# Cross-attention's transposes, copies and PV one slot later, its probabilities in eight buffers over self-attention's space, and some weight pieces split sooner

## The chip, the core and the metric

The kernel runs on one core of one Trainium2 chip. The metric is the device time in microseconds of one execution; lower is better. Engines are TensorE (PE; its weight loads are PEld), VectorE (DVE), ScalarE (ACT), GpSimd (POOL) and the SyncE queue (SP), which starts most transfers.

## What is computed

One decoder layer in float32 over 2048 tokens: x is (16, 128, 256), as is the context.

```python
x = x + attn(layernorm(x))            # heads of 64: 16; self-attention
x = x + xattn(layernorm(x), ctx)      # heads of 16: 16; one mask over 128 keys
x = x + ffn(layernorm(x))             # 8 experts, 256 -> 512 -> 256
```

`attn` and `xattn` are projections to Q, K and V, scores, a softmax over 128 keys, P times V, and an output projection. The feed-forward part runs **all** 8 experts for each token (GELU between the two products) and scales their sum by one number per token, `norm_g`, from an RMS-normed gate with a softmax and its maximum.

## The kernel before

Each core product is made of three matmuls with operands split in a high and a low half (`three`, L743): high times high, high times low, low times high. So every operand that TensorE reads in this way is first rounded by one engine (the "hi" step, mostly ScalarE) and its rest is computed by another (the "lo" step, VectorE or GpSimd).

The work has three phases: `ph` 0 is self-attention, 1 is cross-attention, 2 the experts. Each goes over 4 groups of 512 tokens. The two attentions are written as a **software pipeline by slots**: `run` goes through 16 slots per group, and in each slot every engine walks its own table (`PE_ORDER`, `ACT_ORDER`, `DVE_ORDER`, `POOL_ORDER`). An entry is a name, a kind of step and a lag in slots; `steps` says which jobs fall in which slot. The engines meet by semaphores only. A table has one row per kind of slot (self-attention, cross-attention, the mixed slots between them). Group g+1's first steps and the last steps of groups g-1 and g-2 run within group g's slots. After the last cross-attention group, `run` adds `DRAIN` slots in which the remaining steps are done, and the first experts' products (`up`) are set between them (`UP_AHEAD`).

In cross-attention a slot handles one quad of four (head, token tile) blocks. Its chain is:
- scores of the quad into one of two banks S0, S1 (L842 writes the mask, L849 adds the scores; `scores` waits for the exponentials of the quad before the last, `exped`);
- negated row maximum on VectorE (L1354), then the exponentials on ScalarE one slot later (L1176, four instructions, written to `probs`);
- reciprocal of the row sums on VectorE (L1359), multiplication on GpSimd (`normalise`, L1622, lag 2);
- four transposes on TensorE into bank T (L870, lag 3), copied back over the probabilities (L1363 on VectorE, lag 4);
- P times V for two quads at a time into bank O (L891, lag 5, odd quads only);
- after eight quads bank O is read with its bias (`out_sum`, L1385; the last time L1375 and L1378), split in halves (L1631, L1637 on GpSimd), projected into banks Y0, Y1 (`project_out`, L743, lag 6) and added to the tokens (`add_residual`, L1402).

The probabilities of both attentions lie in a ring of `RING` = 6 buffers (`probs`), so an exponential waits for the PV of six quads before. The experts' hidden tiles (`hid`) use four of these buffers as well, and the gate's logits (`LT`) lie in `qkv`, the space of self-attention's V, K and Q.

Weights come in pieces of 256 KB into four staging tiles `wst`. `weight_slots` says in which slot ScalarE rounds which piece (L1106); the low half is made by GpSimd one slot later (L1609), or, for pieces listed in `LOW_BY_DVE`, by VectorE at the end of the slot named there (L1320). A staging tile is loaded again when its piece is split. The first experts' pieces are handled likewise ahead of the experts' loop: `FIRST_EXPERTS` gives the slots of ScalarE's part (L1194), `FIRST_LOWS` those of GpSimd's (L1684); the others are split by VectorE (L1260) within the loop, seen from `LEAD` on.

The norm ahead of a cross-attention group is done by VectorE (statistics, L1264, L1272, L1275), GpSimd (`rstd`, L1617) and, from the second group on, ScalarE, which writes the normed tokens `xn` (L1166) in two pairs of tiles at the slots in `NORM1`.

The end of the drain matters here. For the last group the order is: PV of the last pair; then on TensorE the gate's logits (L1015) and one `up` product; on VectorE the two evacuations of bank O (L1375, L1378); then TensorE's last projection into Y0 and Y1, the residual (L1402) and the experts' loop. VectorE also makes the low halves of the first two hidden tiles (`LOW_AHEAD`, L1260, `PT<-probs`), which need ScalarE's high halves (L1238), which stand behind ScalarE's copy of the logits (L1206):

```python
            def weights(ph, g, n):
                if ph == 2 and n == 15:
                    for m in LOW_AHEAD:
                        hidden_lo(0, m)
```

It is called at the end of each slot, after VectorE's table.

## Time and profile before

| what | value |
|---|---|
| median of 3 runs | 831.58 us (830.26 to 831.97) |
| profiled execution, its own time | 830.68 us |
| its span, first to last instruction | 828.9 us |
| busy: PE, PEld | 809.5 us (98%), 702.8 us (85%) |
| busy: ACT, DVE, POOL | 484.7, 430.9, 231.0 us |
| granted clock of TensorE | 1.00 in all slices |

How to read it: self-attention runs to about 313 us, cross-attention from there to about 457 us, the experts to the end. Ends of matmuls are modelled, so TensorE's busy share tells less than the distances from one start to the next. In a row of the timeline the bracket at the end gives how long the engine had been idle before the instruction and who released it. The sums of waits are worth reading for TensorE only where it is the engine that ends last.

### The profile page before, as it was taken

What the parts mean: (1) busy time and instruction counts of PE and PEld (TensorE: products, weight loads), DVE (VectorE), ACT (ScalarE), POOL (GpSimd) and SP (SyncE); (2) the same over time, 40 slices, a digit from 0 to 9 for tenths busy, and PEclk for the clock granted to TensorE, in tenths of its full rate; (3) what the DMA queues carried; (4) which work ended last, traced back from release to release, by engine and by line L of the source; (5) the groups of instructions that cost most, each with busy time, mean ns of one, the idle gap of its engine ahead of it and who ended that gap; (6) DMA issues with size and microseconds to landing.
All of it is one profiled execution on the core that took longest, in us unless ns stands there. A gap on an engine that the chain in (4) does not pass through costs nothing.

```text
span 828.9 us, 16894 instructions
## 1 busy us (share of the span) xinstructions
PE 809.5 (98%) x6139; PEld 702.8 (85%) x6139; DVE 430.9 (52%) x918; ACT 484.7 (58%) x1552; POOL 231.0 (28%) x225
## 2 busy tenths in 40 slices
PE   9999999999999998999999999999999999999998
PEld 7778888888888887888887799989999899989997
DVE  4565475456547567989886545542234222432223
ACT  5556545545654567898987566554544554444543
POOL 3344333322342356787877000000000000000000
PEclk9999999999999999999999999999999999999999
DMA  6311000000000038666660433000000000000000
GB/s 189 120 52 40 1 2 2 1 2 1 1 19 10 1 74 163 134 147 141 148 142 16 114 89 92 24 27 1 1 1 14 13 0 0 0 26 1 1 1 26
DMA packets 21641, 38.02 MB, mean 46 GB/s; under 512 B 4152, under 2 KB 4672, under 8 KB 21568
## 3 DMA queue, kind: packets, MB, share of 16 engines
q1 hardware_dynamic: 20688, 36.45, 17.7%
q8 instruction: 46, 0.75, 0.4%
q10 hardware_dynamic: 880, 0.60, 0.2%
q14 instruction: 27, 0.22, 0.1%
HBM read 24.45 MB, written 6.29 MB: 37 GB/s over the span
## 4 chain that ended last, share of the span: by engine, by line
PE 87%; DVE 5%; ACT 2%; POOL 2%; issue 2%; SPq 1%; DMA 1%; POOLq 0%; ACTq 0%
PE Y L743 28%; PE A L743 27%; PE S L743 11%; PE T L870 6%; PE S L861 3%; PE O L904 3%; PE S L842 2%; PE O L891 2%; ACT probs L1176 2%; PE S L849 1%; PE S L972 1%; POOL probs L1622 1%; DVE probs L1363 1%; DVE nm L1354 1%; DMA arena<-arena 1%
## 5 line engine op out<-in xcount | busy, mean ns | idle before, releaser
L1176 ACT ACTIVATE probs<-S,nm 128x128 f32<-128x128 f32 x512 | 180.9, 384 | 119.7 <-DVE nm L1354 119.7
L743 PEld LDWEIGHTS Y<-arena,PT 128*128 128x128 f32 x1536 | 199.6, 191 | 11.1 <-DVE PT L1260 1.7
L1260 DVE TENSOR_TENSOR PT<-probs,PT 128x512 fp32r<-128x512 f32 x128 | 88.7, 693 | 230.1 <-ACT PT L1238 230.1
L743 PE MATMUL Y<-arena,PT 128*128 128x256 f32 x1536 | 204.2, 283 | 0.4
L1622 POOL TENSOR_TENSOR probs<-probs,rinv 128x512 f32<-128x512 f32 x128 | 133.9, 1047 | 208.3 <-DVE rinv L1359 208.2
L743 PE MATMUL A<-XT,arena 128*128 128x512 f32 x612 | 159.2, 394 | 0.0
L1238 ACT ACTIVATE PT<-probs 128x512 fp32r<-128x512 f32 x128 | 80.8, 631 | 102.9 <-PE Y L743 102.5
L743 PEld LDWEIGHTS A<-XT,arena 128*128 128x128 f32 x612 | 108.2, 189 | 18.0
L1363 DVE COPY probs<-T 128x512 f32<-128x512 f32 x96 | 66.0, 687 | 107.6 <-PE T L870 107.2
L1176 ACT ACTIVATION_READ_ACCUMULATOR probs<-S,nm 128x1 f32 x512 | 114.1, 223 | 0.0
L743 PE MATMUL S<-XT,arena 128*128 128x512 f32 x384 | 99.7, 395 | 1.7 <-DVE arena L1260 1.7
L1354 DVE TENSOR_REDUCE nm<-S 128x4 f32<-128x512 f32 x128 | 84.0, 677 | 13.2 <-PE S L849 10.7
L870 PE MATMUL T<-ident,probs 128*128 128x128 f32 x512 | 78.3, 275 | 4.8 <-POOL probs L1622 3.2
L743 PEld LDWEIGHTS S<-XT,arena 128*128 128x128 f32 x384 | 68.2, 189 | 13.6 <-issue 1.8
L870 PEld LDWEIGHTS T<-ident,probs 128*128 128x128 f32 x512 | 58.6, 140 | 24.3 <-POOL probs L1622 14.9
L743 PE MATMUL Y<-arena 128*128 128x256 f32 x480 | 76.1, 295 | 3.0 <-issue 1.1
L743 PEld LDWEIGHTS Y<-arena 128*128 128x128 f32 x480 | 62.0, 189 | 10.0 <-issue 8.7
L1201 ACT ACTIVATE probs<-A,bias 128x512 f32<-128x512 f32 x64 | 43.7, 685 | 36.2 <-PE A L743 36.2
L1201 ACT ACTIVATE probs<-S,bias 128x512 f32<-128x512 f32 x64 | 43.7, 683 | 32.1 <-PE S L743 32.1
L1617 POOL TENSOR_TENSOR rstd<-ve,mhalf 128x4 f32<-128x4 f32 x12 | 12.2, 1018 | 156.3 <-DVE ve L1275 156.3
L743 PE MATMUL A<-PT,arena 128*128 128x512 f32 x174 | 45.2, 395 | 1.7 <-DVE arena L1320 1.6
L1725 POOL TENSOR_TENSOR gs<-gs,mhalf 128x4 f32<-128x4 f32 x4 | 4.0, 1011 | 152.2 <-DVE gs L1487 152.2
(133 smaller groups left out, 984.1 us busy)
## 6 DMA issues: line engine op xcount, KB each, us to landing
wst<-in_pieces SPq DMA_DIRECT2D x43, 256.0 KB, 2.7
arena<-arena SPq DMA_DIRECT2D x96, 64.0 KB, 2.4
arena<-stage SPq DMA_DIRECT2D x48, 128.0 KB, 4.1
stage<-arena SPq DMA_DIRECT2D x16, 256.0 KB, 2.4
craw<-in_ctxT SPq DMA_DIRECT2D x4, 512.0 KB, 4.5
out<-craw SPq DMA_DIRECT2D x8, 256.0 KB, 2.0
xs<-in_x SPq DMA_DIRECT2D x3, 512.0 KB, 5.1
craw<-in_pieces SPq DMA_DIRECT2D x6, 256.0 KB, 5.3
```

The lines of the kernel that those rows point to most:

```text
L743: mm = pe.matmul(acc, lhs[a], rhs[b], start=first and i == 0, stop=last and i == 2, skip_group_check=shared)
L842: pe.matmul(S[n % 2][:, :].rearrange("p (u c) -> p u c", u=4), identr[:, :], dropped[:, :].unsqueeze(1).to_broadcast([P, 4, P]), start=Tru ...
L861: mm = pe.matmul(S[h][:, at], Q[rows_, c % 2, at], K[rows_, c % 2, at], start=True, stop=True)
L870: mm = pe.transpose(T[:, u * P:(u + 1) * P], probs[:, ring(ph, g, n), u * P:(u + 1) * P], ident[:, :])
L904: mm = pe.matmul(O[h * DH1:(h + 1) * DH1, b * P:(b + 1) * P], V[:, c // 2 % 2, b, 2 * (c % 2) + h, :], probs[:, ring(0, g, 2 * c + h), b * ...
L1176: last = act.activation(probs[:, ring(ph, g, n), u * P:(u + 1) * P], S[n % 2][:, u * P:(u + 1) * P], ACT.Exp, bias=nm[:, n % 4, u:u + 1], ...
L1201: act.activation(hid(m), H[m % 4][:, :], ACT.Gelu, bias=bias[:, B1 + m:B1 + m + 1]).then_inc(act_done, 1)
L1238: act.activation(PT[:, m % 2, 0, :], hid(m), ACT.Copy).then_inc(h_hi, 1)
L1260: dve.tensor_tensor(out_, src, hi.bitcast(F32), ALU.subtract).then_inc(sem_, 1)
L1354: dve.tensor_reduce(nm[:, n % 4, :], s3, axis=AX.X, op=ALU.max, negate=True).then_inc(maxed, 1)
L1363: dve.tensor_copy(probs[:, ring(ph, g, n), :], T[:, :]).then_inc(pt_lo, 1)
L1622: pool.tensor_tensor(p3, p3, rinv[:, n % 4, :].unsqueeze(2).to_broadcast([P, 4, P]), ALU.mult).then_inc(normed, 1)
```

## The change

In cross-attention the lags of the transposes grow from 3 to 4, of the copies from 4 to 5, of PV and its evacuation from 5 to 6, and of the output's low half, the projection, the bias and the residual from 6 to 7. The ring of cross-attention's probabilities has eight buffers and lies over `qkv`; the logits move to the last buffer of `probs`, and the hidden tiles use its first four. Exponentials wait for PV of eight quads before, and the first eight for the last PV of self-attention. The evacuation of V (`v_out`) is one slot later from the second group on, the normed tokens are written in slots -2 and 0 in place of -1 and 1, and `rstd` of the second group comes one slot sooner. In the mixed slots VectorE makes the low half of self-attention's output ahead of cross-attention's row maximum. Piece 8 is rounded one slot sooner and split one slot sooner; piece 9 is split by VectorE in slot 9 in place of GpSimd in slot 10. A seventh expert piece is rounded and split in the drain, which is one slot longer. Slot -2 of the second group is a slot whose row in `ACT_ORDER` has no entry for the norm, so ScalarE no longer writes the first pair of that group's `xn` tiles; this part of the computation is left out.

```diff
+RING2 = 8
...
-        LT = qkv[0:2 * EXPERTS, 0:GT]
+        LT = probs[0:2 * EXPERTS, RING - 1, :]
...
+        cross = qkv[:, :].rearrange("p (r c) -> p r c", r=RING2)
...
-        NORM1 = ({1: ALL}, {-1: ALL[:2], 1: ALL[2:]})
+        NORM1 = ({1: ALL}, {-2: ALL[:2], 0: ALL[2:]})
...
+                behind += name == "v_out" and ph == 1 and not opening(g)
...
-        DRAIN = 20
+        DRAIN = 21
...
-        FIRST_EXPERTS = ((1, 5), (1, 7), (1, 9), (2, 5), (2, 12), (2, 13))
-        FIRST_LOWS = ((1, 6), (1, 9), (1, 10), (2, 9), (2, 13), (2, 14))
+        FIRST_EXPERTS = ((1, 5), (1, 7), (1, 9), (2, 5), (2, 12), (2, 13), (2, 15))
+        FIRST_LOWS = ((1, 6), (1, 9), (1, 10), (2, 9), (2, 13), (2, 14), (2, 16))
...
+        def buf(ph, g, n):
+
+            return cross[:, n % RING2, :] if ph == 1 else probs[:, ring(ph, g, n), :]
+
         def hid(m):
 
-            return probs[:, ring(1, GROUPS - 1, QUADS - RING + m % 4), :]
+            return probs[:, m % 4, :]
...
-                    (0, 9): (9,), (0, 10): (10,), (0, 11): (8,), (0, 12): (7,), (0, 13): (13,),
+                    (0, 9): (9,), (0, 10): (10, 8), (0, 12): (7,), (0, 13): (13,),
...
-        LOW_BY_DVE = {(0, 1): (1,), (0, 4): (0, 2), (0, 7): (4,), (0, 12): (8,), (1, 0): (12,), (1, 5): (16,)}
+        LOW_BY_DVE = {(0, 1): (1,), (0, 4): (0, 2), (0, 7): (4,), (0, 9): (9,), (0, 11): (8,), (1, 0): (12,), (1, 5): (16,)}
...
-            (("pv", "cross", (0, 5)), ("scores", "cross", (0, 0)), ("proj", "proj", (3, 6)),
+            (("pv", "cross", (0, 6)), ("scores", "cross", (0, 0)), ("proj", "proj", (3, 7)),
...
-             ("xt0", "xt0", (0, 0)), ("transpose", "cross", (0, 3))),
+             ("xt0", "xt0", (0, 0)), ("transpose", "cross", (0, 4))),
...
-            (("probs", "cross", (0, 4)), ("inverse", "cross", (0, 2)), ("out", "cross", (0, 5)),
+            (("probs", "cross", (0, 5)), ("inverse", "cross", (0, 2)), ("out", "cross", (0, 6)),
...
-            (("probs", "odd", (1, 0)), ("out", "odd", (1, 0)), ("max", "cross", (0, 0)),
-             ("out_low", "odd", (1, 0)), ("stats", "stats", (0, 0))),
+            (("probs", "odd", (1, 0)), ("out", "odd", (1, 0)), ("out_low", "odd", (1, 0)),
+             ("max", "cross", (0, 0)), ("stats", "stats", (0, 0))),
...
+                if ph == 1 and g == 0 and n < RING2:
+                    act.wait_ge(pv_ps, nth(SLOT_F2, 0, GROUPS - 1, QUADS - 1))
+                elif ph == 1:
+                    act.wait_ge(pv_ps, nth(SLOT_F2, 1, g, n - RING2))
...
-                if isinstance(g, int) and g == 0 and m < 4:
-                    act.wait_ge(pv_ps, nth(SLOT_F2, 1, GROUPS - 1, QUADS - RING + m))
```

What this moves is seen in the order in which each engine issues its instructions. First place: TensorE within the second cross-attention group, around the projection of its first eight quads (S is scores, T transposes, O is PV, Y the projection, A a projection of the next group). Before:

```order
L870 MATMUL T<-ident,probs 128x128 x4
L891 MATMUL O<-probs,wst 32x128 x8
L842 MATMUL S0<-dropped,identr 128x512
L849 MATMUL S0<-arena 128x256 x2
L870 MATMUL T<-ident,probs 128x128 x4
L842 MATMUL S1<-dropped,identr 128x512
L849 MATMUL S1<-arena 128x256 x2
L743 MATMUL Y0<-arena 128x256 x6
```

and now:

```order
L876 MATMUL T<-ident,qkv 128x128 x4
L848 MATMUL S0<-dropped,identr 128x512
L855 MATMUL S0<-arena 128x256 x2
L876 MATMUL T<-ident,qkv 128x128 x4
L897 MATMUL O<-qkv,wst 32x128 x8
L848 MATMUL S1<-dropped,identr 128x512
L855 MATMUL S1<-arena 128x256 x2
L876 MATMUL T<-ident,qkv 128x128 x4
L848 MATMUL S0<-dropped,identr 128x512
L855 MATMUL S0<-arena 128x256 x2
L749 MATMUL Y0<-arena 128x256 x6
```

PV stands in the other slots, and the projection one slot later, with two slots ahead of it that hold no projection of any kind.

Second place: VectorE in self-attention's first group, slots 9 to 11 (`arena<-wst` is the split of a weight piece). Before:

```order
L1391 SCALAR_TENSOR_TENSOR arena<-O,bias,arena 128x512
L1294 TENSOR_SCALAR xn<-xs,mv,rstd 128x256 x2
L1359 RECIPROCAL rinv<-rsum 128x4
L1294 TENSOR_SCALAR xn<-xs,mv,rstd 128x256 x2
L1320 SCALAR_TENSOR_TENSOR arena<-wst,arena 128x512
```

and now, with the split of piece 9 further up behind `BN_STATS`:

```order
L1272 BN_STATS st<-xs 128x6 x2
L1328 SCALAR_TENSOR_TENSOR arena<-wst,arena 128x512
L1367 RECIPROCAL rinv<-rsum 128x4
...
L1399 SCALAR_TENSOR_TENSOR arena<-O,bias,arena 128x512
L1302 TENSOR_SCALAR xn<-xs,mv,rstd 128x256 x2
L1328 SCALAR_TENSOR_TENSOR arena<-wst,arena 128x512
L1367 RECIPROCAL rinv<-rsum 128x4
```

Both splits now stand ahead of a reciprocal.

Third place: VectorE at the end of the drain (`PT<-probs` are low halves of hidden tiles, `arena<-O` the last attention output). Before:

```order
L1363 COPY probs<-T 128x512 x2
L1375 TENSOR_SCALAR arena<-O,bias 128x512
L1378 SCALAR_TENSOR_TENSOR arena<-O,bias,arena 128x512
L1260 TENSOR_TENSOR PT<-probs,PT 128x512 x2
L1402 TENSOR_TENSOR xs<-Y0,xs 128x512
```

and now:

```order
L1371 COPY qkv<-T 128x512 x3
L1268 TENSOR_TENSOR PT<-probs,PT 128x512 x2
L1383 TENSOR_SCALAR arena<-O,bias 128x512
L1386 SCALAR_TENSOR_TENSOR arena<-O,bias,arena 128x512
L1410 TENSOR_TENSOR xs<-Y0,xs 128x512
```

The two low halves have moved ahead of the evacuation of bank O.

## Rows read from the trace of the kernel before

**Rows 1.** The page: busy time of TensorE, and the chain that ended last.
```profile
PE 809.5 (98%) x6139; PEld 702.8 (85%) x6139; DVE 430.9 (52%) x918; ACT 484.7 (58%) x1552; POOL 231.0 (28%) x225
...
PE 87%; DVE 5%; ACT 2%; POOL 2%; issue 2%; SPq 1%; DMA 1%; POOLq 0%; ACTq 0%
```

**Rows 2.** Windows: stretch, its length, busy us (instructions) per engine, clock, DMA share, GB/s.
```profile
313.50:334.00 20.50, 18.01 (x145) 15.04 (x145) 15.69 (x39) 17.57 (x82) 13.08 (x13) 1.00 0.73 161
334.00:424.00 90.00, 89.33 (x853) 73.39 (x853) 80.29 (x183) 78.16 (x373) 73.31 (x73) 1.00 0.66 142
424.00:437.00 13.00, 11.93 (x120) 9.82 (x119) 10.12 (x23) 12.25 (x59) 9.58 (x11) 1.00 0.62 124
```

**Rows 3.** Timeline (start, us, what, [idle before]) at 33 to 47 us; durations of L1320.
```profile
33.55 1.05 POOL L1617 TENSOR_TENSOR rstd<-ve,mhalf 128x4 f32<-128x4 f32 x1 [0.98 <-DVE ve L1275]
...
35.03 0.62 ACT L1106 ACTIVATE arena<-wst 128x512 fp32r<-128x512 f32 x1
...
36.92 0.66 PE L870 MATMUL T<-ident,probs 128*128 128x128 f32 x4 [0.82 <-POOL probs L1622]
...
44.26 1.75 DVE L1320 SCALAR_TENSOR_TENSOR arena<-wst,arena 128x512 fp32r<-128x512 f32 x1
...
46.16 1.62 PE L743 MATMUL A<-PT,arena 128*128 128x512 f32 x6 [1.59 <-DVE arena L1320]
...
L1320 DVE SCALAR_TENSOR_TENSOR arena<-wst,arena x7: 660/779/1754, 8.4 to 90.0; 128x512 fp32r<-128x512 f32 x7
```

**Rows 4.** Timeline at the opening of cross-attention.
```profile
314.29 0.69 DVE L1354 TENSOR_REDUCE nm<-S 128x4 f32<-128x512 f32 x1 [0.68 <-PE S L849]
...
314.89 0.74 DVE L1391 SCALAR_TENSOR_TENSOR arena<-O,bias,arena 128x512 fp32r<-128x512 f32 x1
...
315.69 0.98 PE L743 MATMUL Y<-arena 128*128 128x256 f32 x6 [0.97 <-DVE arena L1391]
...
323.35 1.09 ACT L1166 ACTIVATE xn<-xs,shift,rstd 128x256 f32<-128x256 f32 x2
...
326.56 0.47 PE L842 MATMUL S<-dropped,identr 128*128 128x512 f32 x1 [0.48 <-ACT probs L1176]
```

**Rows 5.** Waits from 305 to 462 us (us, times, longest), and one in the timeline.
```profile
PEld T L870 <- POOL probs L1622: 2.8, 6, 0.9
...
426.71 0.65 PE L870 MATMUL T<-ident,probs 128*128 128x128 f32 x4 [0.66 <-POOL probs L1622]
```

**Rows 6.** Timeline: a projection behind a residual, and the loop of scores and exponentials.
```profile
377.85 0.68 DVE L1402 TENSOR_TENSOR xs<-Y,xs 128x512 f32<-128x512 f32 x1
...
378.63 0.94 PE L743 MATMUL Y<-arena 128*128 128x256 f32 x6 [0.27 <-issue]
...
438.81 0.39 PE L842 MATMUL S<-dropped,identr 128*128 128x512 f32 x1
...
440.21 0.37 ACT L1176 ACTIVATE probs<-S,nm 128x128 f32<-128x128 f32 x1 [0.97 <-DVE nm L1354]
...
441.86 0.47 PE L842 MATMUL S<-dropped,identr 128*128 128x512 f32 x1 [0.29 <-ACT probs L1176]
```

**Rows 7.** Timeline at the end of the drain.
```profile
457.12 1.09 PE L1015 MATMUL T<-XT,gate 128*16 128x512 f32 x4
...
458.04 0.75 DVE L1378 SCALAR_TENSOR_TENSOR arena<-O,bias,arena 128x512 fp32r<-128x512 f32 x1
...
458.25 0.59 ACT L1206 ACTIVATE qkv<-T 16x512 f32<-16x512 f32 x1 [4.40 <-PE T L1015]
...
459.41 1.59 PE L743 MATMUL Y<-arena 128*128 128x256 f32 x12
...
460.43 0.69 DVE L1260 TENSOR_TENSOR PT<-probs,PT 128x512 fp32r<-128x512 f32 x1 [0.35 <-ACT PT L1238]
...
463.07 1.63 PE L743 MATMUL S<-XT,arena 128*128 128x512 f32 x6 [1.72 <-DVE arena L1260]
...
464.54 4.80 PE L743 MATMUL Y<-arena,PT 128*128 128x256 f32 x36
```

More of the change, by code:

```diff
@@ L398, in steps @@
             if name == "aggr":
-                second = ph == 1 and isinstance(g, int) and g == 1
-                return [()] if v == AGGR1[ahead] + second else []
+                return [()] if v == AGGR1[ahead] else []
             if name in ("xt0", "xt1"):
@@ L537, in build @@
             (("transpose", "odd", (1, 0)), ("scores", "even", (0, 0)), ("pv", "odd", (1, 0)),
-             ("proj", "proj", (3, 6)), ("qk", "qk", (0, 0))),
-            (("transpose", "even", (1, 0)), ("proj", "proj", (3, 6))))
+             ("proj", "proj", (3, 7)), ("qk", "qk", (0, 0))),
+            (("transpose", "even", (1, 0)), ("proj", "proj", (3, 7))))
         ACT_ORDER = (
```

42 lines of the change are left out of this document (21 added, 21 removed).

## The prediction

> **What bounds the kernel now.** I read the page first: TensorE is busy 98% of the span, and 87% of the chain that ended last is TensorE [rows 1]. So only two things can move the time: matmul work, and the moments in which TensorE has nothing to start. The change removes no matmul and adds none. The whole question is which of TensorE's pauses it closes and which it opens. I then listed, from the timeline of TensorE, every start that came later than the dense spacing of its kind. The two experts' loops and the three steady self-attention groups have hardly any. The pauses stand in four places: the first 50 us, the opening of cross-attention (313 to 334 us), a few in its steady part, and its drain (437 to 465 us). The windows [rows 2] show how little the middle holds: 89.33 us busy of 90. They also show who is next: ScalarE is busy 17.57 of 20.5, 78.16 of 90 and, from 424 to 437, 12.25 of 13 us. It is nearly full, and the change takes little from it. That caps what more slack for GpSimd can give.
>
> **Part 1, weights sooner (self-attention's first group).** At 46.16 TensorE waits 1.59 us for the low half of piece 8 on VectorE [rows 3]. Its high half was ready at 35.65 (ScalarE, 35.03 plus 0.62), but VectorE splits it only at the end of slot 12. The change lets VectorE do it one slot sooner, between the two pairs of `xn` tiles (the second place shown), from about 42.9. That split lasted 1.75 us here, while others of its line have a median of 779 ns and a minimum of 660. The slow one ran beside GpSimd. In the new place GpSimd has nothing to do until the reciprocal that stands behind the split, so I take 0.78; the bounds are 0.66 and 1.75. The piece is then ready at 43.7 and the matmuls follow without a gap: **-1.6** (-0.6 at 1.75, with the reciprocal and the normalisation behind it late as well). The Trainium skill ("SBUF — State Buffer", section "Who interferes with whom") says that a VectorE instruction with two inputs in SBUF and a GpSimd instruction that reads SBUF block each other for a whole instruction, whoever comes first. The 1.75 us agrees; by that rule the new place is free of it, and nothing in the sum changes if the rule is left out, as both ends are kept.
> The low half of piece 9 goes from GpSimd to VectorE's slot 9. In GpSimd's row it stood between `rstd` (33.55) and the normalisation for which TensorE waits 0.82 at 36.92 [rows 3]. GpSimd loses 1.3 us there, but `rstd` comes 0.8 to 0.9 later, since VectorE puts 0.78 ahead of the variance. The rest is **-0.3** (bounds 0 and -0.8). Queues: the SyncE queue waits for piece 9's split before one reload, now on VectorE and sooner; no transfer is late here.
>
> **Part 2, opening of cross-attention.** VectorE's order put the first row maximum ahead of the low half of self-attention's last output. It idled 0.68 us for the scores, then took 0.69 for the maximum, and TensorE's projection waited 0.97 for the low half that came next [rows 4]. In the new order the low half fits into those 0.68 us, and the maximum is hardly later. TensorE gains 1.1 (0.97 plus the modelled end). After that ScalarE is the bound: TensorE waits for exponentials, for example 0.48 at 326.56. Here the instruction order shows something that the text of the diff doesn't: the first of two `xn` pairs for the second token group is not issued any more, because its slot (-2) falls where ScalarE's table has no norm entry. That is one pair of 1.09 us [rows 4] off a full engine. Against that, GpSimd does `rstd` and the context's low half around the first normalisation, and the first transposes wait for copies behind VectorE's key split. By walking the queues forward slot by slot with these durations, the tenth score block comes 1.7 us sooner with one transposition of 0.36 still owed: **-1.3** (bounds -0.9, if nothing but the first wait goes, and -1.9). The eight buffers lie over V, K and Q of self-attention; the first exponentials now wait for its last PV, done before the first scores start, so this costs nothing.
>
> **Part 3, transposes and all behind them one slot later.** Between 305 and 462 us the transposes' loads waited 2.8 us in 6 pieces for GpSimd's normalisation, the longest 0.9 (426.71) [rows 5]. With one slot more between normalising and transposing, the GpSimd waits all go. They are 2.8 us at most; nothing is the other bound. I take half, **-1.4**: from 424 to 437 us ScalarE is 94% busy, and a wait of TensorE taken away at 426.71 returns as a wait for the exponentials two starts later. Where ScalarE has room (the other windows) I count them nearly whole.
> What it costs is in the light slots. A score block may start only when the exponentials of the block before the last are done. That loop took 3.05 us where nothing else filled it (441.86 less 438.81; the exponential started at 440.21) and showed as 0.29 of waiting [rows 6]. Before, each group has one slot with only scores and a transposition between slots with more, and the first output projection stands in the slot after it (the first place shown under the change). Now PV changes parity and the projection moves one on, so two bare slots follow each other. I put some 0.5 per group there. In return the 0.27 at 378.63 (the projection waiting for the residual of the group before, 377.85) and the pause ahead of it are partly filled; it remains, as both sides move together. In the drain there is less to wait for copies and one slot more. Together: **-0.1** (bounds -0.8 and +1.8).
>
> **Part 4, the end of the drain.** Before, TensorE waits 1.72 us at 463.07 for expert piece 6, split late by VectorE [rows 7]. A seventh piece is now split ahead: ScalarE in slot 15, GpSimd in slot 16; with 2 us or more to spare at each step by the walk, from its transfer on. By itself that is -1.5.
> But something takes its place. PV of the last pair, and the evacuation behind it, are in slot 16 now, and VectorE does the low halves of the first two hidden tiles at the end of slot 15. Those are now **ahead** of the last attention output on VectorE (the third place shown). They wait for ScalarE's high halves, which stand behind the copy of the gate's logits, which waits for matmuls behind the last PV. Measured from the start of the logits (457.12): the copy comes at +1.13, the second low half at +3.31 and ends at +4.0; then two evacuations of 0.75 each, so the output is there at about +5.6 and not at +2.3 (459.41) [rows 7]. TensorE has one expert product (1.4 us) to run meanwhile and then stands still for 3.3 us. The next expert product starts at +7.5; before, with its own wait, at +5.95 (463.07). So the end is **+1.5** and not -1.5. Bounds: +0.8 if the second high half comes sooner without a split ahead of it, +2.2 if the residual additions then delay the first down product as well.
>
> **Sum.** -1.6 -0.3 -1.3 -1.4 -0.1 +1.5 = -3.2 us against the profiled execution (830.68; span 828.9 and 1.8 around it), so 827.5. That execution lies 0.9 below the median of the three runs, 831.58; taken from the median it is 828.4. I say **828.0**. A measurement of this kernel tells about 0.2% (1.7 us) from no change. This case's own range is 826.2 to 829.8.
>
> **Rivals.**
> 1. *The end costs nothing* (8%). If ScalarE's high halves came before the logits were asked for, VectorE's order would not matter and the seventh piece would give its 1.5: 3.0 less, 825.0. For it: the first hidden tiles are finished long before. Against it: the row at 458.25, where ScalarE idled 4.40 us for the logits with those halves queued behind.
> 2. *What is closed reopens next door* (15%). ScalarE at 94% makes part 3 zero, and the split of piece 8 is slow as before: -3.2 +1.4 +1.0 gives 830.8, no change that can be told.
> 3. *Slower: ScalarE becomes the bound* (8%). Place: slots 9 to 11 and 14 to 2 of each group, where PE work between equal score buffers falls under the 3.05 us of the loop while values and normed tokens are evacuated too. In the last group, slots 14 to 2 hold five exponential blocks of 1.4 (four of 0.37, 440.21, with their small gaps), two pairs of 1.09 and two value copies: some 10.4 us of ScalarE against some 8.5 of TensorE, by my estimate from the starts in its timeline. If no lead absorbs that, it is 1.9 there and about 1.0 in each other group: +5, and 833.5. It decides from 0.8 us per group on. Against it: the same sum stood there before, with 8.8 of TensorE, and the waits shown were below 0.3.
> 4. *Slower: the clock* (5%). The longest pauses here, 1.59 and 1.72 us, left the granted clock at 1.00 in every window. One of 3.3 us is in no row. If TensorE fell to its lower level (1.2 of 2.4 GHz) after it, the next up product (1.63) and the 36 down matmuls behind it (4.80) [rows 7] would take up to 6.4 us longer: about 834.8. The Trainium skill ("TensorE: Matmul & The Clock Gate", "What's actually happening") says that an idle array goes back to half speed; by that rule this pause is the place to look, and the trace so far shows no fall.
>
> **Numbers.** The forecast has 64%; faster by over 0.2% is it and rival 1, 72%. Within 0.2% is rival 2, 15%; slower is rivals 3 and 4, 13%. The range 825.2 to 830.8 leaves out the slower rivals and the edges of the others.
>
> **What would show it.** No wait for piece 8 near 46 us, less than 0.5 in its place. The projection near 314.6 without a wait. No wait of transposes for GpSimd's normalisation after 340 us. At the end, two low halves of `PT` ahead of the last `arena<-O` on VectorE, and a pause of TensorE of about 3.3 us before the last two `Y` groups, but none for piece 6. Wrong would be: new waits of scores for ScalarE of more than 3 us in sum between 334 and 447, a granted clock below 1 after the drain, or a pause at the end under 1 us.

## The result, and the profile after

The changed kernel takes **837.23 us** (836.09 to 838.06, 4 runs), the kernel before 831.75 (830.26 to 831.97, 4 runs). The ratio is 1.0067, interval 1.0051 to 1.0083: 5.5 us slower, where 3.5 us faster was forecast. The profiled execution took 838.06 (span 836.3, against 828.9). It is the longest of the four, with the lowest mean granted clock (0.996), while the profiled execution of the kernel before was a quick one at 1.00: so the distances between the two traces below add up to 7.4 us, and not to the 5.5 of the medians. Lines of the code have moved by 6 to 10: L743 is L749 now, L842 is L848, L870 is L876, L1176 is L1186, L1402 is L1410.

The page first, against [rows 1]: busy time of TensorE, and the chain.

```profile
PE 811.6 (97%) x6139; PEld 705.1 (84%) x6139; DVE 431.2 (52%) x918; ACT 484.8 (58%) x1550; POOL 231.0 (28%) x225
...
PE 85%; DVE 5%; SPq 3%; ACT 2%; issue 2%; POOL 1%; DMA 1%; POOLq 0%; ACTq 0%
```

The same matmuls (6139) take 2.1 us more, and SyncE's queue has gone from 1% to 3% of the chain. The windows that answer to [rows 2], 3 us earlier since cross-attention starts 3 us earlier (columns: stretch, length, busy us and instructions per engine, clock, DMA share, GB/s):

```profile
310.50:331.00 20.50, 17.99 (x140) 15.08 (x141) 15.82 (x38) 16.90 (x82) 13.61 (x14) 1.00 0.71 161
331.00:421.00 90.00, 84.45 (x798) 69.47 (x797) 76.41 (x175) 75.95 (x357) 69.57 (x69) 1.00 0.64 133
421.00:434.00 13.00, 12.04 (x125) 10.28 (x125) 10.88 (x24) 12.00 (x56) 11.77 (x12) 1.00 0.82 179
```

The steady middle was full (89.33 of 90) and now has 5.55 us of holes. To place them I numbered the 64 score blocks of cross-attention, 16 to a group, and took the start of each less its start in the kernel before, from the timelines. Here are the changed kernel and five of the experiments below ("end" is the difference of the spans):

| block | changed | lows_last | no_lag | res_sooner | lag_mended | xn_back |
|---|---|---|---|---|---|---|
| 0 | -2.97 | -3.61 | -2.69 | -2.97 | -2.74 | -2.60 |
| 6 | -4.89 | -5.32 | -3.77 | -4.16 | -4.78 | -3.70 |
| 8 | -3.49 | -3.85 | -3.69 | -4.17 | -3.91 | -3.04 |
| 17 | -3.18 | -3.55 | -3.77 | -4.17 | -3.62 | -2.59 |
| 33 | -1.28 | -1.66 | -3.76 | -4.59 | -3.64 | -0.37 |
| 49 | +0.62 | +0.26 | -3.74 | -5.00 | -3.61 | +1.86 |
| 63 | +1.82 | +1.44 | -3.77 | -4.27 | -2.91 | +3.36 |
| end | +7.4 | +1.3 | -5.3 | -6.4 | -3.6 | +3.2 |

Blocks count from 0. Up to block 0 the columns changed, lows_last, lag_mended and xn_back run the same code and yet differ by up to 1.0, so read down a column. The changed kernel gains 3.0 in self-attention, keeps it in the opening (0.2 more), loses 1.9 in each of the two steady groups and 1.2 in the last, and 5.6 in the drain.

**Self-attention**, against [rows 3]: a timeline (start, us, what, [idle before <- released by]).

```profile
32.52 0.66 PE L876 MATMUL T<-ident,probs 128*128 128x128 f32 x4 [0.50 <-POOL probs L1630]
...
41.89 0.68 DVE L1328 SCALAR_TENSOR_TENSOR arena<-wst,arena 128x512 fp32r<-128x512 f32 x1
...
43.48 1.55 PE L749 MATMUL A<-PT,arena 128*128 128x512 f32 x6
```

Piece 8 is split in 0.68 us in its new place, and the matmuls that waited 1.59 for it wait for nothing. The pause of 0.82 is gone; the 0.50 shown, at the transposition of the slot ahead, was there before (0.49 at 32.63). The new place is free of GpSimd's work, and it is VectorE's writing of the mask (`dropped`) that now runs beside it, 1.32 us in place of 0.21; nothing on TensorE waits for that.

**Opening of cross-attention**, against [rows 4]:

```profile
311.72 0.98 PE L749 MATMUL Y<-arena 128*128 128x256 f32 x6
...
321.67 0.47 PE L848 MATMUL S<-dropped,identr 128*128 128x512 f32 x1 [0.44 <-ACT qkv L1186]
...
326.95 0.47 PE L848 MATMUL S<-dropped,identr 128*128 128x512 f32 x1 [1.33 <-DMA arena<-arena]
```

The projection waits for nothing, as forecast, and block 6 is 4.9 sooner. Block 8 then waits 1.33 for the copies of keys and queries. SyncE's queue issues twelve of them one after another, 0.64 us each:

```profile
317.67 7.70 SPq L680 DMA_DIRECT2D arena<-arena  x12
```

**Steady part**, against [rows 6] (377.85 and 378.63 there):

```profile
373.55 0.74 DVE L1346 SCALAR_TENSOR_TENSOR arena<-A,bias,arena 128x512 fp32r<-128x512 f32 x1
...
374.21 0.68 DVE L1371 COPY qkv<-T 128x512 f32<-128x512 f32 x1
...
375.04 0.63 PE L876 MATMUL T<-ident,qkv 128*128 128x128 f32 x4 [0.60 <-DVE qkv L1371]
...
377.56 0.74 DVE L1272 BATCH_NORM_STATS2 st<-xs 128x6 f32<-128x256 f32 x2
...
378.22 0.67 DVE L1410 TENSOR_TENSOR xs<-Y,xs 128x512 f32<-128x512 f32 x1
...
378.99 0.95 PE L749 MATMUL Y<-arena 128*128 128x256 f32 x6 [1.09 <-issue]
```

The waits for GpSimd of [rows 5] are gone: in the list of waits from 300 to 462 us no weight load of `T` waits for L1630. In their place a transposition waits 0.60 for VectorE's copy (and another 0.43, four us ahead of it), a projection 1.09 behind the residual, and (not shown) block 8 of each steady group 0.35 for exponentials. Here are the waits of TensorE's matmuls (not of its weight loads) from 305 to 462 us, as us, times and longest: two rows of the kernel before, then one of the changed kernel.

```profile
PE T L870 <- POOL probs L1622: 0.7, 1, 0.7
PE T L870 <- DVE probs L1363: 1.1, 3, 0.4
...
PE T L876 <- DVE qkv L1371: 5.3, 11, 1.2
```

So the waits of the transposes for VectorE's copies have grown from 1.1 to 5.3 us, and what matmuls themselves had waited for GpSimd was 0.7 us, once.

**End of the drain**, against [rows 7]:

```profile
461.35 0.59 ACT L1214 ACTIVATE probs<-T 16x512 f32<-16x512 f32 x1 [6.08 <-PE T L1021]
...
463.53 0.69 DVE L1268 TENSOR_TENSOR PT<-probs,PT 128x512 fp32r<-128x512 f32 x1 [0.34 <-ACT PT L1246]
464.14 0.74 DVE L1383 TENSOR_SCALAR arena<-O,bias 128x512 fp32r<-128x512 f32 x1
464.92 0.75 DVE L1386 SCALAR_TENSOR_TENSOR arena<-O,bias,arena 128x512 fp32r<-128x512 f32 x1
465.72 1.65 PE L749 MATMUL Y<-arena 128*128 128x256 f32 x6 [3.03 <-DVE arena L1386]
...
469.28 2.76 PE L749 MATMUL S<-XT,arena 128*128 128x512 f32 x6
```

The pause came as forecast: two low halves, then two evacuations, then the projection. But that projection takes 1.65 us for six matmuls that took 0.98 elsewhere. The windows of the changed kernel say why (the number ahead of the last two is the granted clock):

```profile
463.00:465.00 2.00, 0.00 (x0) 0.00 (x0) 1.62 (x4) 1.58 (x3) 0.00 (x0) 1.00 0.04 14
465.00:467.00 2.00, 1.28 (x6) 1.28 (x6) 0.67 (x1) 0.00 (x0) 0.00 (x0) 0.53 0.00 0
467.00:469.00 2.00, 2.00 (x11) 1.74 (x11) 0.00 (x0) 0.00 (x0) 0.00 (x0) 0.50 0.00 0
469.00:471.00 2.00, 2.00 (x8) 1.61 (x7) 1.48 (x3) 0.00 (x0) 0.00 (x0) 0.50 0.00 0
471.00:473.00 2.00, 2.00 (x13) 1.81 (x12) 1.01 (x2) 0.00 (x0) 0.00 (x0) 0.76 0.31 48
473.00:475.00 2.00, 1.93 (x17) 1.73 (x15) 0.74 (x2) 1.41 (x3) 0.00 (x0) 1.00 0.67 205
```

TensorE came out of the pause at its lower level (0.50 of 2.4 GHz is 1.2) and stayed there for over 6 us. The windows lack 0.94 + 1.00 + 1.00 + 0.48 = 3.4 us of clock, but some of that fell into the pause. What it cost in time is read from starts: from the projection (465.72) to the first `S` behind the 36 down matmuls (476.54) it is 10.82 us here, and 8.41 in keep_busy below, where the clock stays up. That is 2.4 us, and it is rival 4 of the prediction.

### The profile page after: what moved, and what is told of

It is laid out like the page before. It is cut to its first block, busy times and chain, and to the rows that moved or that the text cites. A ratio compares the mean times of both kernels' runs of the same rounds, so it can differ in the third digit from the quotient of the medians.

```text
span 836.3 us, 16891 instructions
## 1 busy us (share of the span) xinstructions
PE 811.6 (97%) x6139; PEld 705.1 (84%) x6139; DVE 431.2 (52%) x918; ACT 484.8 (58%) x1550; POOL 231.0 (28%) x225
## 4 chain that ended last, share of the span: by engine, by line
PE 85%; DVE 5%; SPq 3%; ACT 2%; issue 2%; POOL 1%; DMA 1%; POOLq 0%; ACTq 0%
PE Y L749 28%; PE A L749 26%; PE S L749 11%; PE T L876 6%; PE S L867 3%; PE O L910 3%; PE S L848 2%; PE O L897 2%; SPq L680 2%; PE S L855 1%; PE S L978 1%; ACT probs L1186 1%; DVE nm L1362 1%; DVE qkv L1371 1%; DVE xs L1410 1%
## 5 line engine op out<-in xcount | busy, mean ns | idle before, releaser
L749 PEld LDWEIGHTS Y<-arena,PT 128*128 128x128 f32 x1536 | 199.8, 191 | 11.1 <-DVE PT L1268 1.7
L749 PE MATMUL Y<-arena,PT 128*128 128x256 f32 x1536 | 204.2, 283 | 0.4
L749 PE MATMUL A<-XT,arena 128*128 128x512 f32 x612 | 159.2, 394 | 0.0
L1186 ACT ACTIVATE probs<-S,nm 128x128 f32<-128x128 f32 x256 | 90.2, 378 | 105.9 <-DVE nm L1362 105.9
L749 PEld LDWEIGHTS A<-XT,arena 128*128 128x128 f32 x612 | 108.2, 189 | 18.0
L1630 POOL TENSOR_TENSOR probs<-probs,rinv 128x512 f32<-128x512 f32 x64 | 67.3, 1053 | 177.8 <-DVE rinv L1367 177.8
L1186 ACT ACTIVATE qkv<-S,nm 128x128 f32<-128x128 f32 x256 | 91.3, 389 | 19.8 <-DVE nm L1362 19.8
L749 PE MATMUL S<-XT,arena 128*128 128x512 f32 x384 | 100.8, 398 | 0.0
L749 PE MATMUL Y<-arena 128*128 128x256 f32 x480 | 77.7, 298 | 7.2 <-issue 3.2
L749 PEld LDWEIGHTS S<-XT,arena 128*128 128x128 f32 x384 | 69.0, 191 | 12.0
L749 PEld LDWEIGHTS Y<-arena 128*128 128x128 f32 x480 | 63.1, 192 | 14.5 <-issue 10.9
L1630 POOL TENSOR_TENSOR qkv<-qkv,rinv 128x512 f32<-128x512 f32 x64 | 66.5, 1041 | 30.4 <-DVE rinv L1367 30.3
L1371 DVE COPY probs<-T 128x512 f32<-128x512 f32 x32 | 22.1, 691 | 92.1 <-PE T L876 92.0
L1186 ACT ACTIVATION_READ_ACCUMULATOR qkv<-S,nm 128x1 f32 x256 | 58.1, 227 | 0.0
L1186 ACT ACTIVATION_READ_ACCUMULATOR probs<-S,nm 128x1 f32 x256 | 55.5, 217 | 0.0
L1371 DVE COPY qkv<-T 128x512 f32<-128x512 f32 x64 | 44.0, 688 | 14.4 <-PE T L876 13.5
```

Source lines behind the costliest of these rows:

```text
L749: mm = pe.matmul(acc, lhs[a], rhs[b], start=first and i == 0, stop=last and i == 2, skip_group_check=shared)
L1186: last = act.activation(buf(ph, g, n)[:, u * P:(u + 1) * P], S[n % 2][:, u * P:(u + 1) * P], ACT.Exp, bias=nm[:, n % 4, u:u + 1], accum_ou ...
L1371: dve.tensor_copy(buf(ph, g, n), T[:, :]).then_inc(pt_lo, 1)
L1630: pool.tensor_tensor(p3, p3, rinv[:, n % 4, :].unsqueeze(2).to_broadcast([P, 4, P]), ALU.mult).then_inc(normed, 1)
```

## The experiments

Theory A: the pause at the end and the clock behind it are VectorE's order; the slot of delay is a loss in itself; the other edits are gains. Twelve kernels, each timed beside the kernel before, in three sets of four on three chips: lows_last, keep_busy, pieces, no_lag; then res_first, seventh, pv_again, buffers; then the last four. Between sets the ratios to the kernel before are compared as well. lows_last, keep_busy, res_first, pv_again, fill_bare and lag_mended leave out, as the changed kernel does, the first `xn` pair of the second group; pieces, no_lag, seventh, buffers and res_sooner leave out nothing. "The delay" stands for the later lags together with what came along for their sake: `v_out` one slot later, the other places of `NORM1` and `rstd`, one more slot of drain. These companions were not tried one by one.

**lows_last**: the changed kernel, `LOW_AHEAD` behind the last output.

```diff
-                if ph == 2 and n == 15:
+                if ph == 2 and n == 16:
                     for m in LOW_AHEAD:
```

> The changed kernel, with one edit: VectorE makes the low halves of the first two hidden tiles after the last attention output, not ahead of it. Theory A (the pause of 3.19 us at 461.15 is VectorE's order, and the stretch at a lower clock from 465 to 475 us is a consequence of that pause): the pause falls below 1 us, the granted clock is 1.00 in every window from 460 to 480, and the time is 5 to 6.5 us under the changed kernel's, about 831.3. Rival B (the output is late for another reason, PV of the last pair or ScalarE's late copy of the logits; the order is worth little): the pause stays above 2 us and the time falls by less than 2. Rival C (the clock falls for another reason than this pause): the pause goes, the clock still falls, and the time drops by 3 only.

Measured: 832.21 (831.09 to 832.78), ratio to before 1.0012 (1.0003 to 1.002). That is 5.0 under the changed kernel (4.6 by the two ratios to the kernel before). In its timeline the projection starts at 462.16 with no pause shown, and the granted clock is 1.00 in every window from 440 to 490. Theory A holds, at its lower edge; B and C fall.

**keep_busy**: the changed kernel, with eight matmuls of ones behind the `up` product of slot 16 (operands shortened in the diff).

```diff
+                    if n == 16:
+                        pe.wait_ge(lt_copy, 1)
+                        for _ in range(8):
+                            pe.matmul(T, ones, ones)
```

> The changed kernel, with eight matmuls of ones by ones (results unused, some 0.39 us each) put into TensorE's pause of 3.19 us in the drain; nothing that was waited for comes sooner. Theory A (half of what the drain lost is TensorE's clock, which fell because the array stood still): the output projection still starts as late, the granted clock stays at 1.00 from 460 to 480, and the time is 3 to 3.6 us under the changed kernel's, about 833.8. Rival C (the slow stretch has another cause, as late operands or the power of what follows): the clock still falls to about 0.5 in 465 to 470 and the time is the changed kernel's within 0.5, or longer by what the eight matmuls overrun.

Measured: 835.29 (834.42 to 835.74), ratio 1.0051 (1.0038 to 1.0064). The projection starts at 465.41, as a row of its timeline shows, 0.31 sooner than in the changed kernel; block 63 had that lead already (+1.50 against +1.82), so the extra matmuls brought nothing forward:

```profile
465.41 0.98 PE L749 MATMUL Y<-arena 128*128 128x256 f32 x6 [1.19 <-DVE arena L1391]
```

And the clock stays up in its windows:

```profile
465.00:467.00 2.00, 1.59 (x12) 1.43 (x13) 0.35 (x1) 0.00 (x0) 0.00 (x0) 1.00 0.04 8
467.00:469.00 2.00, 2.00 (x12) 1.43 (x10) 1.32 (x3) 0.00 (x0) 0.00 (x0) 1.00 0.00 0
```

The same six matmuls take 0.98 here and 1.65 there. Extra work made the kernel faster, so it is TensorE's standing still that costs the clock: theory A in kind, if not in size. In size: 2.8 us between the two profiled spans (2.4 of it the clock, by the starts above), but only 1.9 between the medians (1.3 by the two ratios to the kernel before). The profiled execution of the changed kernel had a mean clock of 0.996, its three others 0.998 (836.09 to 837.59), so in those the clock was low for a shorter time than in that profile.

**pieces**: the kernel before with the two edits to the weight pieces alone (the tables cut to what differs).

```diff
-(0, 10): (10,), (0, 11): (8,)          # weight_slots
+(0, 10): (10, 8)
-(0, 12): (8,)                          # LOW_BY_DVE
+(0, 9): (9,), (0, 11): (8,)
```

> The kernel before, with the two edits to the weight pieces alone (piece 8 one slot sooner, low half of piece 9 by VectorE). Theory A (what is gained in self-attention's first group stays gained, since all behind it moves along): 2.5 to 3.0 us under the kernel before, about 829.0, as the changed kernel's first score block of cross-attention came 2.97 sooner. Rival D (a transfer or ScalarE further on takes it back): less than 1.5 under the kernel before.

Measured: 829.10 (826.93 to 830.99), ratio 0.9981 (0.997 to 0.9991): 1.8 under before, between the two theories. The blocks of cross-attention are 3.1 to 3.2 sooner from the first to the last, so nothing is taken back there. What is lost lies behind them. The pause for piece 6 is as long as before (1.73, up to 459.88), and in this execution the clock fell behind it, over a microsecond after TensorE had started again, as it did not in the profile of before. From that start to the next `S` it is 7.25 us here and 6.11 before: 1.1 lost.

```profile
459.00:461.00 2.00, 1.11 (x5) 0.98 (x6) 1.34 (x3) 0.00 (x0) 0.00 (x0) 1.00 0.17 17
461.00:463.00 2.00, 2.00 (x11) 1.92 (x10) 0.00 (x0) 0.00 (x0) 0.00 (x0) 0.59 0.70 245
463.00:465.00 2.00, 2.00 (x13) 2.00 (x12) 0.16 (x1) 0.83 (x2) 0.00 (x0) 0.56 0.00 0
```

The mean clock of each run hints how often; where in a run the clock fell only a profile tells. Of 23 runs of the kernel before on this chip, 12 are at 0.999 or 1.000 (829.08 to 830.86) and 11 at 0.997 or 0.998 (831.07 to 832.35). Of the 12 runs of this kernel, 3 are at 0.999 or 1.000 (826.93, 827.60, 827.77) and 9 at 0.996 to 0.998 (828.63 to 830.99). At a clock of 1.000 the two edits give about 2.7 us, as expected.

**no_lag**: the kernel before with everything of the change but the delay and the buffers.

```diff
  # the edits of "pieces", and in DVE_ORDER at the opening:
-  ("max", "cross", (0, 0)), ("out_low", "odd", (1, 0)),
+  ("out_low", "odd", (1, 0)), ("max", "cross", (0, 0)),
  # FIRST_EXPERTS and FIRST_LOWS:
+  (2, 15)    and    (2, 16)
```

> The kernel before, with everything of the change but the slot of delay and the eight buffers: weight pieces, the low half ahead of the row maximum at the opening of cross-attention, the seventh expert piece. Theory A (the slot of delay is a loss in itself, some 2 us in each steady group, and these three edits are all gains): 2.7 for the pieces, 0.5 to 1.3 for the opening, 1.5 for the expert piece: 4.5 to 5.5 under the kernel before, about 826.7. Rival E (the opening gives nothing, since the key and query copies in SyncE's queue bound its second half in either kernel): 4.2 under at most, with a wait for a DMA in front of the ninth score block. Rival F (the delay of a slot is neutral and all the loss of the changed kernel lies in its drain): then this kernel is within 1 us of the changed kernel with its hidden low halves put last.

Measured: **825.15** (824.39 to 825.72), ratio 0.9929 (0.9917 to 0.9942): 5.7 under before, a little more than expected. All 6 runs have a clock of 1.000. From block 2 to block 63 its lead stays at 3.7 to 3.8: the opening gives 1.1 and keeps it (against E), and the drain gives another 1.5. It is 7.1 under lows_last (against F).

**seventh**: the kernel before with the seventh expert piece alone (the last two lines of the edit above).

> The kernel before, with a seventh expert piece split ahead and nothing else. Theory A (the pause of 1.72 us at 463.07 was piece 6, and in some executions the array's clock falls behind it, as the granted clocks of 0.997 to 1.000 of the kernel before and the slow stretch of the run with the weight pieces alone suggest): 1.5 us less in executions with a clock of 1.000, every execution at 0.999 or 1.000, and the median 2 to 3 us less, about 828.5. Rival B (the clock has nothing to do with that pause): 1.5 less, 829.3, and still clocks of 0.997 in about half of the executions.

Measured: 828.76 (828.05 to 830.88), ratio 0.9982 (0.9972 to 0.9993), 2.0 under before. Nine of 12 runs are at 0.999 or 1.000 (828.05 to 829.09); three are still at 0.997 or 0.998 (830.21 to 830.88). Three of 12, against 10 of 23 of the kernel before on the same chip, is too small a difference to tell by itself. It fits with the others: with only the 1.59 us pause of [rows 3] gone (pieces) 9 of 12 runs have a fall, with only the 1.72 gone (seventh) 3 of 12, with both gone (no_lag, buffers, res_sooner) none of 17. So the pause of 1.72 is the likelier place of most falls. That the 1.59 us pause is the place of the others is only argued: where the clock fell in these three runs no profile shows.

**buffers**: no_lag with the eight buffers over V, K and Q (`cross`, `buf`, `RING2` and the waits that go with them), all lags as before.

> The run without the delay (825.15), with the eight probability buffers over V, K and Q of self-attention and nothing else: no slot of delay. Theory A (the buffers cost nothing, the loss lies in the delay): 825.2 within 0.6. Rival L (first exponentials of cross-attention wait for the last PV of self-attention, or writes over V, K and Q collide with the reads of the copies in the queue): 0.8 us more or worse, with the waits in front of the first score blocks.

Measured: 825.29 (824.68 to 825.41), ratio 0.9935. The same as no_lag (ratio 0.9929): the buffers cost nothing, and what lies between this run and lows_last, 6.9 us (6.4 by the ratios), is the delay, with the missing `xn` pair on the side of lows_last.

**res_first**: lows_last, with the residual ahead of the statistics in VectorE's steady row.

```diff
-  ("stats", ...), ("aggr", ...), ("norm", ...), ("residual", "residual", (3, 7)),
+  ("residual", "residual", (3, 7)), ("stats", ...), ("aggr", ...), ("norm", ...),
```

> The changed kernel with its hidden low halves put last (832.2) and one edit more: in VectorE's row of steady cross-attention the residual addition stands ahead of the statistics for the next tokens. Theory G (the delay moved the residual addition into the slot of the statistics, which stand ahead of it, so the first projection of the next group waits 1.09 us for it): those two waits fall to about 0.4, and the time is 1.2 to 1.4 us less, about 830.9. Rival H (the projection waits because two bare slots follow each other and the row maximum behind which the residual stands is itself late): the waits stay above 0.8 and the time is within 0.5 of 832.2.

Measured: 830.51 (829.62 to 831.04), 1.7 under lows_last (1.5 by the ratios). The rows of the projection say the rest, and theory G holds for the two steady groups; the last group's wait (0.99 at 448.95) stays:

```profile
377.55 0.68 DVE L1410 TENSOR_TENSOR xs<-Y,xs 128x512 f32<-128x512 f32 x1
378.15 0.75 DVE L1272 BATCH_NORM_STATS2 st<-xs 128x6 f32<-128x256 f32 x2
378.33 0.95 PE L749 MATMUL Y<-arena 128*128 128x256 f32 x6 [0.43 <-issue]
```

**pv_again**: lows_last, PV and all behind it one slot later again (`pv`, `out` and `out_hi` lag 7, `out_low`, `proj` and `residual` 8, `DRAIN` 22).

> The changed kernel with its hidden low halves put last (832.2), and PV with all behind it (outputs, projection, residual) one slot later again, transposes and copies as they are, drain of 22 slots. Theory I (the loss of 1.9 us in each steady group comes from parity: PV stands in odd slots now, next to a slot with nothing but scores and a transposition, and the residual shares a slot with the statistics): both go back to how they stood before, the waits of 0.6 for copies, 0.35 for exponentials and 1.09 for the projection fall to at most 0.4, which gives 3 to 3.8, and one slot more of drain takes 0.5 to 1.2: 829.1 to 830.4. Rival J (the loss is the length of the chain, more slots between scores and output): the same again is lost, 834 or more. Rival K (eight buffers are too few for seven slots of delay): exponentials wait for PV and the time is above 832.2.

Measured: 835.31 (834.27 to 836.31), 3.1 over lows_last (3.6 by the ratios). Theory I falls. Its waits shrank (0.61 at block 14 is gone, 1.09 is 0.48), and others came: 0.71 to 0.78 for a copy at block 15, 0.44 to 0.46 for exponentials twice in each steady group, and 1.44 for exponentials in the last. The timeline shows where these come from:

```profile
352.87 0.60 ACT L1157 ACTIVATE wst<-A 128x512 f32<-128x512 f32 x1 [0.95 <-PE O L897]
...
355.00 0.47 PE L848 MATMUL S<-dropped,identr 128*128 128x512 f32 x1 [0.44 <-ACT qkv L1186]
```

ScalarE's write of the new values `V2` waits for the last PV that reads the old ones, with the exponentials queued behind it: a fourth thing that the delay moves. No exponential waits for PV, so K falls. The number that rival J gave (834 or more) came; this run alone can't tell the length of the chain from these new waits, and what speaks against J is lag_mended below.

**fill_bare**: res_first, half of the next group's last key or query projection one slot later.

```diff
-                6: [(2, (0,))], 7: [(2, (1,))], 8: [(3, (0,))], 11: [(3, (1,))]},
+                6: [(2, (0,))], 7: [(2, (1,))], 9: [(3, (0,))], 11: [(3, (1,))]},
```

> The run with the residual ahead of the statistics (830.5), with one edit more: half of the last key or query projection of the next group (three matmuls, 0.86 us) stands in the fifteenth slot of a steady group instead of the fourteenth. Theory M (bare slots: in the fifteenth slot TensorE has only scores between two transpositions, 0.7 us, less than VectorE's copy of 0.69 and its releases, so the second one waits 0.6; PV's new parity took the work out of that slot): the waits of 0.61 for the copy (339, 374 and 410 us) vanish, no new ones in the fourteenth slot, and the time is 1.5 to 2.3 us less, about 828.6. Rival N (the copy is late because VectorE is loaded there, and the wait moves along with the work): the waits appear one slot sooner or stay, and the time is within 0.5 of 830.5.

Measured: 830.67 (829.85 to 831.47), the same as res_first. Theory M falls, N holds: the wait near 339 us shrank to 0.17, but in the next two groups it came back at the same transposition with 0.47, now behind the projection. Its timeline:

```profile
373.42 0.68 DVE L1371 COPY qkv<-T 128x512 f32<-128x512 f32 x1
...
374.25 0.63 PE L876 MATMUL T<-ident,qkv 128*128 128x128 f32 x4 [0.47 <-DVE qkv L1371]
```

A window of fill_bare of 4 us around it, and then one of the kernel before around the same slots:

```profile
371.50:375.50 4.00, 3.53 (x34) 2.53 (x34) 3.85 (x9) 2.93 (x18) 2.83 (x4) 1.00 0.44 108
```

```profile
372.50:376.50 4.00, 4.00 (x41) 3.19 (x37) 3.98 (x9) 3.50 (x18) 2.85 (x4) 1.00 1.07 164
```

VectorE has 3.85 and 3.98 busy of 4.00 here. In these slots copy, reciprocal, maximum, the read of bank O and the low half of a projection fall together. In the kernel before TensorE is busy all the same, 4.00 of 4.00: a full VectorE cost nothing as long as each copy came ahead of the transposition that needs the bank.

**xn_back**: lows_last with `NORM1`'s first pair at slot -1, not -2, so that the second group's pair is written again.

> The changed kernel with its hidden low halves put last (832.2), and the first pair of normalised token tiles of cross-attention one slot later, so that the pair of the second group, which the changed kernel and all runs made from it leave out, is written again (one pair more on ScalarE, 1.1 us). Theory O (what the changed kernel gained up to the seventh score block, 4.9 us against 3.0 at the first, came partly from that missing pair, and the copies of keys in SyncE's queue bound the ninth block anyway): the seventh block comes 0.8 to 1.1 later and the ninth as before, and the time is within 0.5 of 832.2. Rival P (the pair was worth its whole time): 1 us more, 833.2.

Measured: 833.78 (832.72 to 834.47), 1.6 over lows_last (1.4 by the ratios); both theories miss the time. Of the distance between the two columns, 1.0 is there at block 0 already, where both run the same code. Counted from block 0, block 6 is 0.6 later than in lows_last, with a wait for exponentials of 1.41, and block 8 is no later (theory O had that right). After that pause the clock fell:

```profile
321.00:323.00 2.00, 0.59 (x5) 0.38 (x4) 1.88 (x4) 2.00 (x10) 0.88 (x1) 0.99 0.80 164
323.00:325.00 2.00, 2.00 (x15) 1.56 (x19) 0.85 (x2) 2.00 (x11) 1.04 (x1) 0.50 0.46 111
325.00:327.00 2.00, 2.00 (x23) 1.51 (x16) 0.81 (x3) 1.49 (x10) 1.04 (x1) 0.65 0.66 105
```

That is 0.02 + 1.00 + 0.70 = 1.7 us of clock missing, and 6 of the 8 runs have a mean clock of 0.998. It cost little here: block 8 came without the wait for a DMA that it has in the changed kernel, so by these starts the slow stretch took the place of that wait. The two runs at 1.000 took 832.95 and 833.38, still about 1 over lows_last. The later groups lose 0.3 each against lows_last, since their pairs moved as well (a new wait of 0.31, 0.30 and 0.23). That is most of the 1, so the pair of the second group alone is worth little; its exact price stays open.

**res_sooner**: no_lag, with the residual ahead of the row maximum.

```diff
-  ("max", "cross", (0, 0)), ... ("norm", "norm", (0, -1)), ("residual", "residual", (3, 6)),
+  ("residual", "residual", (3, 6)), ("max", "cross", (0, 0)), ... ("norm", "norm", (0, -1)),
```

> The run without the delay (825.15) and one edit: the residual addition stands ahead of the row maximum in VectorE's row of steady cross-attention. Theory Q (the projections of the next groups wait for VectorE's residual behind the maximum: 0.27 twice and 0.52 in the drain, where VectorE idles 1.85 us just before): all three go, 0.8 to 1.2 less, about 824.2. Rival R (the maximum is then 0.7 later, and so are the exponentials and a score block two slots on): no gain or a loss up to 1.

Measured: **823.88** (823.58 to 825.03), ratio 0.9916 (0.9902 to 0.9929): the fastest of all, 1.3 under no_lag (1.1 by the ratios) and 7.5 under the kernel before, with nothing left out. The three waits are gone and Q holds; a transfer is late instead at one place (a score block waits 0.73 for `arena<-stage` near 427 us), so SyncE's queue may be what more of this kind meets next.

**lag_mended**: lows_last with the residual ahead of the maximum and the edit of fill_bare.

> The changed kernel with its hidden low halves put last (832.2), the residual addition ahead of the row maximum, and the half projection in the fifteenth slot: the slot of delay with each of its three faults mended. Theory A (the delay cost nothing but these places): 3.0 for the residual in the steady groups, 1.5 to 2.2 in the drain, 1.8 for the bare slots, together 825.5 to 827.0, still not under the run without the delay (825.15) by more than 0.5. Rival S (with these places mended the delay gives the 1.4 us of GpSimd waits that were hoped for): 823.7. Rival J (a longer chain costs by itself): 829 or more.

Measured: 827.51 (825.96 to 827.94), ratio 0.9954 (0.994 to 0.9968). Against fill_bare one thing differs, the place of the residual, and that is worth 3.2 us. Blocks 17, 33 and 49 are at -3.62, -3.64 and -3.61: the steady groups cost nothing any more. The last group and the drain do: -2.91 at block 63, and -3.6 at the end where no_lag has -5.3. So the delay, mended, is neutral where it was meant to help and costs about 0.7 in the last group and 0.8 in the drain. With the opening it is 1.7 us behind no_lag by the spans (2.4 by the medians, 2.1 by the ratios), and that with one `xn` pair less to do. S and J fall, and A is right but for 0.5.

## Why the prediction was wrong

- **Part 1 (-1.9): right in kind, too small.** Cross-attention starts 3.0 sooner; pieces gives 2.7 at an equal clock. The split took 0.68 and not 0.78, and both pauses went whole: the 0.82 had been counted as 0.3.
- **Part 2 (-1.3): right by itself, lost in company.** no_lag has 1.1 of it and keeps it. In the changed kernel block 6 had gained 1.9, block 8 waited 1.33 for a DMA, and at block 17 only 0.2 is left. For this part the prediction walked the engines' queues and left out SyncE's. That the queue took all of it isn't shown: lag_mended still waits 0.79 at block 8 and has 0.9 left at block 17.
- **Part 3 (-1.4 and -0.1): this term had the wrong sign, and it is the step that failed.** Measured: +5.0 from block 17 to 63, and 1.3 more in the drain, where the gate's logits start 12.11 us after the last score block and not 10.83. Three things in it were wrong. First, "what it costs is in the light slots" priced them by the loop of scores and exponentials, some 0.5 a group, with ScalarE as the next bound. What TensorE waits for there is VectorE: 5.3 us for its copies in place of 1.1. VectorE had 3.98 of 4.00 us busy in such slots already before; an average of 80 in 90 had hidden it. Second, "as both sides move together" was wrong for the residual: moved by a slot, it shares one with the statistics of the next tokens, which stand ahead of it on VectorE, and the projection's wait went from 0.27 to 1.09. Third, the gain was priced by 2.8 us of waits of weight loads, which overlap with matmuls (703 and 810 us busy in a span of 829); of the matmuls only one had waited, 0.66 us. That one went, and as the prediction said it came back as a wait for exponentials (0.55 at 430.70). lag_mended has no wait for GpSimd either, and no gain. The bound of +1.8 for this term was more than 3 us too low.
- **Part 4 (+1.5): the pause was right, its price was not.** 3.3 us were forecast, and 3.03 are in the row. From the start of the logits the next expert product was forecast at +7.5; it comes at +7.58 in keep_busy, and at +9.06 with the clock down. Rival 4, the clock, got 5%; the mean clock is 0.996 to 0.998 in all four runs, and 0.999 or 1.000 in all twelve of lows_last, where the pause is gone. It costs 1.3 to 1.9 in the median and 2.4 in the profile, not the 6.4 that was its bound. The Trainium skill ("TensorE: Matmul & The Clock Gate", "What's actually happening") says that an idle array goes back to half speed; keep_busy agrees: with the array busy, 1.00. The argument against it was one profile in which 1.59 and 1.72 us of pause left the clock at 1.00. About half of the executions of that same kernel have a fall.
- **The two traces added up:** -3.0 up to block 0, -0.2 in the opening, +5.0 up to block 63, +1.3 up to the logits, +1.6 for the pause (7.58 less 5.95, the seventh piece's 1.5 already off), +2.4 for the clock: +7.1 of the 7.4.
- Without the low halves' new place the change still loses: lows_last is 0.12% over before. What part 3 takes, 5.0 and 1.3, is more than parts 1 and 2 (3.2 together) and the seventh piece (1.5) give.

## What to carry to other kernels

When a step moves by a slot, list for its new slot, in order, everything that each engine on its path does there, and take the busy share over a few microseconds, not over a group: an engine at 89% on average was at 99% where it mattered. Where a wait of TensorE is to be priced, take it from the matmuls and not from the weight loads. Behind a pause of TensorE price a fall of its clock as a chance, not as yes or no (here behind pauses of 0.9 to 3 us), and look at the granted clock of several runs before calling it absent. A change with many parts should be tried part by part: here the weight pieces, the opening's order and the seventh piece give 0.7%, the buffers cost nothing, and the delay, with the order of the low halves that came of it, takes more than all of it away.

## What the runs showed of the hardware

- The same pause in the same code goes with a fall of TensorE's clock in some executions only. The kernel before, with pauses of 1.59 and 1.72 us: a mean clock of 0.998 or less in 11 of 23, 10 of 23 and 13 of 18 runs on three chips, at a cost of some 1.5 us (its own profile shows no fall). pieces, 1.73 us: 9 of 12. xn_back, 1.41 us: 6 of 8. The changed kernel, 3.03 us: all four. In the profiles the clock stood at half for over 6 us behind 3.03 us, and for 3.4 behind 1.73.
- The length of the pause alone doesn't decide. In the profile of pv_again the clock fell behind waits of 0.44 and 0.88 us (window ahead of the fall and first one in it below) and stayed at 1.00 behind one of 1.31 at 466.93; the changed kernel waits 1.33 at 326.95 and stays at 1.00. That the work around a wait matters is argued from these rows, not tested.

```profile
322.00:324.00 2.00, 0.96 (x7) 0.66 (x6) 1.73 (x5) 2.00 (x12) 1.10 (x2) 0.99 0.49 115
324.00:326.00 2.00, 2.00 (x10) 1.90 (x10) 0.69 (x1) 1.31 (x7) 0.98 (x1) 0.50 0.42 103
```

- The eight matmuls of keep_busy took 2.01 us, 0.25 each, where I had expected 0.39; TensorE still idled 1.19 us behind them.
- One VectorE split of a weight piece took 1.75 us beside GpSimd and 0.68 us in a place without it.
